# Edge loop of a graph layer: a group's matrix products over three turns, and one ranking step for four tiles in place of two

## The reference

```python
env = 0.5 * (jnp.cos(d * jnp.pi / CUTOFF) + 1.0) * (d < CUTOFF)
rbf = jnp.exp(-0.5 * ((d[:, None] - centers) / (jnp.abs(widths) + EPS_W)) ** 2)
r = _silu(rbf * env[:, None] @ rbf_w1 + rbf_b1) @ rbf_w2 + rbf_b2
W = _silu(r @ filt_w1 + filt_b1)
W = _silu(W @ filt_w2 + filt_b2) @ filt_w3 + filt_b3
msg = (x[col] @ node_w + node_b) * W
agg = jax.ops.segment_sum(msg, row, num_segments=x.shape[0])
...
x = layernorm(x + gated(layernorm(x + agg)))
# second layer: the same edges, x summed forth by src and back by dst,
# weighted with the edge weight, divided by the degrees, then a layer norm
```

## Time and profile before

| | |
|---|---|
| median of 3 runs | 6074.43 us (6072.81 to 6118.61) |
| profiled execution, own time | 6161.62 us |
| profiled execution, span in the trace | 6159.9 us |
| mean granted PE clock over the span | 0.765 |
| busy: PE / PEld / DVE / ACT / POOL | 60% / 45% / 40% / 26% / 56% |

### The profile page before, as it was taken

One profiled execution on the slowest core, in us unless ns is written; L12 is line 12 of the kernel. 1 busy time (PEld: TensorE's weight loads), 2 busy tenths in 40 slices (PEclk: granted clock), 3 DMA queues, 4 the chain that ended last, 5 costly groups with the idle time before them and its releaser, 6 DMA issues. The chain is left out here.

```text
span 6159.9 us, 77269 instructions
## 1 busy us (share of the span) xinstructions
PE 3684.4 (60%) x16362; PEld 2754.2 (45%) x16363; DVE 2437.0 (40%) x7283; ACT 1598.0 (26%) x4213; POOL 3420.9 (56%) x3664
## 2 busy tenths in 40 slices
PE   7677776776766777676899633333333444444443
PEld 5444544444444544444688533333332444443443
DVE  5444444444444444444223622112222544444446
ACT  3333333333333333333466511111111000000000
POOL 2555555555555555555567466666666555555555
PEclk8888888888888888888999865555555776667666
DMA  7322332332332323232599111111111333332333
GB/s 202 102 91 94 99 101 93 96 101 90 96 100 91 99 91 97 92 100 95 178 289 293 44 43 43 44 43 42 43 44 56 89 81 80 82 81 74 80 81 86
DMA packets 466367, 589.69 MB, mean 96 GB/s; under 512 B 71696, under 2 KB 387088, under 8 KB 466320
## 3 DMA queue, kind: packets, MB, share of 16 engines
q0 software_dynamic: 128512, 318.04, 16.6%
q1 hardware_dynamic: 337808, 271.12, 15.1%
HBM read 392.20 MB, written 196.67 MB: 96 GB/s over the span
## 5 line engine op out<-in xcount | busy, mean ns | idle before, releaser
L520 POOL DMA_INDIRECT s_rows<-arena,adr x784 | 769.5, 982 | 1155.2 <-issue 1128.7
L945 PE MATMUL ps<-f3s,arena 128*128 128x256 f32 x3136 | 924.8, 460 | 343.2 <-ACT arena L633 331.3
L573 POOL DMA_INDIRECT arena<-x_half,idx x832 | 800.9, 963 | 581.7 <-DVE idx L1496 305.8
L560 POOL DMA_INDIRECT d_rows<-arena,adr x832 | 816.9, 982 | 534.4 <-ACT adr L757 245.2
L945 PEld LDWEIGHTS ps<-f3s,arena 128*128 128x128 f32 x3136 | 725.1, 237 | 484.7 <-issue 328.7
L512 POOL DMA_INDIRECT arena<-y_rows,idx x784 | 757.6, 966 | 308.9 <-issue 237.4
L1119 PE MATMUL ps<-arena 128*128 128x128 f32 x1664 | 364.1, 386 | 766.4 <-DVE arena L1503 506.9
L934 PE MATMUL ps<-arena,f2s 128*128 128x512 f32 x1568 | 719.0, 602 | 0.0
L1119 PEld LDWEIGHTS ps<-arena 128*128 128x128 f32 x1664 | 312.8, 281 | 811.1 <-issue 810.5
L1330 DVE TENSOR_TENSOR arena<-arena,ps 128x512 f32<-128x512 f32 x392 | 269.1, 686 | 825.7 <-PE ps L945 399.7
L1455 DVE TENSOR_TENSOR arena<-rec,ps 128x512 f32<-128x512 f32 x208 | 142.9, 687 | 977.9 <-remote 845.5
(11 more groups left out here) (217 smaller groups left out, 5532.7 us busy)
## 6 DMA issues: line engine op xcount, KB each, us to landing
arena<-s_rows SPq DMA_DIRECT2D x104, 1048.0 KB, 5.7
arena<-d_rows SPq DMA_DIRECT2D x52, 1040.0 KB
arena<-wrow SPq DMA_DIRECT2D x392, 64.0 KB
arena<-env_row SPq DMA_DIRECT2D x392, 64.0 KB
d_rows<-arena,adr POOLq DMA_INDIRECT x832
arena<-x_half,idx POOLq DMA_INDIRECT x832
s_rows<-tpl_s SPq DMA_DIRECT2D x98, 131.0 KB
arena<-y_rows,idx POOLq DMA_INDIRECT x784
```

The costliest lines, as they stand in the source:

```text
L520: pool.indirect_dma_start(s_rows, bass.IndirectOffsetOnAxis(ap=adr[b][:, t:t + 1], axis=0), msg[b][:, t, :], None).then_inc(scattered[b], 16)
L560: pool.indirect_dma_start(d_rows, bass.IndirectOffsetOnAxis(ap=adr[b][:, t:t + 1], axis=0), drow[b][:, t, :], None).then_inc(scattered_d[b ...
L573: pool.indirect_dma_start(gath2[b][:, t, :], None, x1_half, bass.IndirectOffsetOnAxis(ap=idx[b % 4][:, t:t + 1], axis=0)).then_inc(gathere ...
L945: last = mm(o, s3[:, k, t * P:(t + 1) * P], f3s[:, k, :], start=False, stop=False, skip_group_check=True)
```

## The change

Two things change in the edge loop.

**Order.** PE's turn becomes `layer4(g)`, `layer23(g+1)`, the ranking step of g+2, `layer1(g+2)`, `layer5(g-1)`. The products of one group, which stood in two turns and a bit, now stand in three: layer 1 two turns ahead, layers 2 and 3 one turn ahead, layer 4 in the turn, layer 5 one turn behind. ACT and DVE follow: ACT's turn is `silu3(g)` with `bias_in(g-1)` between its halves, `silu2(g+1)`, `silu1(g+2)`, `radial(g+3)`, then the staging as before; DVE's is `radial_basis(g+2)`, `product(g+2)`, both halves of `messages(g-1)`, `ranked(g+2)`, `one_hot_rank(g+3)`. `s3`, the input of layer 5, gets a second buffer.

**Ranking.** A group's four tiles are ranked in one step of eight products (columns 392, 294, 196, 98, 294, 196, 98, 392) in place of two steps of four (196, 98, 196, 98); one product on DVE over 392 columns replaces two over 196.

```diff
-            def silu3(g):
-                for m in range(2):
-                    act.wait_ge(l4_mm, 2 * g + m + 1)
-                    A(s3[:, m, :], ps[:, 3 + m, :], ACT.Silu, bias=col[:, 5 + m:6 + m]).then_inc(s3_done, 1)
+            def silu3(g, b, m):
+                if m == 0 and not (fixed(g) and g < 2):
+                    act.wait_ge(l5_mm, 2 * g - 2)
+                act.wait_ge(l4_mm, 2 * g + m + 1)
+                A(s3[b % 2][:, m, :], ps[:, 3 + m, :], ACT.Silu, bias=col[:, 5 + m:6 + m]).then_inc(s3_done, 1)
...
             def act_group(g, q, b):
-                silu2(g)
+                silu3(g, b, 0)
+                if not (fixed(g) and g == 0):
+                    bias_in(g - 1)
+                silu3(g, b, 1)
+                if ahead(g, 1):
+                    silu2(g + 1)
                 if ahead(g, 2):
-                    radial(g + 2, q + (b + 2) // 4, (b + 2) % 4)
+                    silu1(g + 2, b)
+                if ahead(g, 3):
+                    radial(g + 3, q + (b + 3) // 4, (b + 3) % 4)
                 if ahead(g, 4):
                     stage_idx(g + 4, q + 1, b)
                 if ahead(g, 1):
                     stage_rec(g + 1, q + (b + 1) // 4, (b + 1) % 4)
-                    silu1(g + 1, (b + 1) % 4)
-                bias_in(g)
-                silu3(g)
...
+            def rank_step(g, b):
+                pe.wait_ge(hot_done, g + 1)
+                cur, prev = hot_r[b % 2], hot_r[1 - b % 2]
+                if not (fixed(g) and g == 0):
+
+                    pe.wait_ge(prod_done, g)
+                    mm(ps[:, 7, 0:GT * NB2], after_b[:, :], prev, start=False, stop=False, skip_group_check=True)
+                    for k in range(1, GT):
+                        mm(ps[:, 7, 0:(GT - k) * NB2], ones_b[:, :], prev[:, k:GT, :], start=False, stop=False,
+                           skip_group_check=True)
+                for k in range(1, GT):
+                    mm(ps[:, 7, k * NB2:GT * NB2], ones_b[:, :], cur[:, 0:GT - k, :], start=False, stop=False,
+                       skip_group_check=True)
+                mm(ps[:, 7, 0:GT * NB2], before_b[:, :], cur, start=False, stop=False,
+                   skip_group_check=True).then_inc(rank_mm, 1)
...
             def layer4(g):
                 pe.wait_ge(s2_done, 2 * g + 2)
+                if not (fixed(g) and g == 0):
+                    pe.wait_ge(s3_done, 2 * g)
...
             def pe_group(g, q, b):
-                layer23(g, b)
+                layer4(g)
+                if ahead(g, 1):
+                    layer23(g + 1, b + 1)
                 if ahead(g, 2):
-                    rank_step(g + 2, b, 0)
+                    rank_step(g + 2, b)
+                    layer1(g + 2, b)
                 if not (fixed(g) and g == 0):
-                    layer5(g - 1)
-                if ahead(g, 2):
-                    rank_step(g + 2, b, 1)
-                if ahead(g, 1):
-                    layer1(g + 1, b + 1)
-                layer4(g)
+                    layer5(g - 1, b + 1)
...
-            def product(g, b, h):
-                dve.wait_ge(rank_mm, 2 * g + h + 1)
-                if h == 0 and not (fixed(g) and g == 0):
+            def product(g, b):
+                dve.wait_ge(rank_mm, g + 1)
+                if not (fixed(g) and g == 0):
                     dve.wait_ge(rank_done, g)
-                V.tensor_tensor(prod[:, 2 * h:2 * h + 2, :], hot_r[b % 2][:, 2 * h:2 * h + 2, :],
-                                ps[:, 7, 0:2 * NB2].rearrange("p (t n) -> p t n", t=2), ALU.mult).then_inc(prod_done, 1)
+                V.tensor_tensor(prod[:, :, :], hot_r[b % 2], ps[:, 7, 0:GT * NB2].rearrange("p (t n) -> p t n", t=GT),
+                                ALU.mult).then_inc(prod_done, 1)
...
             def dve_group(g, q, b):
                 if ahead(g, 2):
-                    one_hot_rank(g + 2, b)
-                    product(g + 2, b, 0)
+                    radial_basis(g + 2, b + 2)
+                    product(g + 2, b)
                 if not (fixed(g) and g == 0):
-                    messages(g - 1, q + (b + 3) // 4 - 1, (b + 3) % 4, 0)
+                    for h in range(2):
+                        messages(g - 1, q + (b + 3) // 4 - 1, (b + 3) % 4, h)
                 if ahead(g, 2):
-                    radial_basis(g + 2, b + 2)
-                if not (fixed(g) and g == 0):
-                    messages(g - 1, q + (b + 3) // 4 - 1, (b + 3) % 4, 1)
-                if ahead(g, 2):
-                    product(g + 2, b, 1)
                     ranked(g + 2, b)
+                if ahead(g, 3):
+                    one_hot_rank(g + 3, b + 1)
```

51 lines of the change are left out of this document (21 added, 30 removed).

## The result

The changed kernel takes 5762.55 us (5761.64 to 5771.24, 4 runs), the kernel before, on the same chip, 6086.5 (6072.81 to 6118.61, 4 runs): 324 us less, a ratio of 0.943, 95% interval 0.938 to 0.947. The forecast was 135 less. In a later job the ratio was 0.946.

The account below looks back on a forecast made before the run. The edge loop was taken as bound by POOL's burst, PE's late signal, a message and the next burst. Turns from 14.8 to 14.1 us over 196 turns gave 135 us off 6074, so 5939; range 5585 to 6170.

Parts of the forecast that it names:

- The bound: Edge loop: a circle of POOL's burst, PE's late signal, a message and the next burst; 14.8 us a turn before.
- The held turn: Edge-loop turn with layer 5's signals held until after POOL's burst: 14.2 us, or 13.6 if the first half comes through.
- The doubles: Two POOL bursts without a pause, when layer 5's second half comes through: 24.6 to 32.5 us for two turns.
- The ranking step: PE's 1960 columns in place of 1176: 0.35 us a turn more, hidden in layer 5's spare time, so taken as nothing.
- (a): Edge loop: PE's signals come in time and POOL never waits; 10.3 us a turn, 882 us less, 5190; chance 0.05.
- (b): Edge loop: doubles go well again and again; 12.3 us a turn, 490 us less, 5585; chance 0.13.
- (c): Edge loop: held signals pile up in a new pattern, nothing gained; 14.6 to 15.0 us a turn, 6035 to 6115; chance 0.19.
- (d): Edge loop: at a low PE clock layer 5 ends after the release; 333 us more, 6405; chance 0.18.
- POOL's idle in front of scatters near-equal and no 12 us pauses: Sign on POOL: idle falls to about 3.9 us a turn, near-equal each turn, with few 12 us pauses.
- Messages 0.6 apart after a "remote" idle: Sign on DVE: both messages 0.6 us apart after some 4 us idle, about 2 us after the last gather.
- silu3 turns of 13.5 to 14.3: Sign on ACT: edge-loop turns, read from silu3, lie between 13.5 and 14.3 us.
- Clock 0.9: Sign on PE: the clock in the edge loop is 0.9 or more.

Follow-up runs that it names:

- e1: Kernel before with one ranking step of eight products in place of two of four, in a job without late signals: 1.000 of the kernel before.
- f2: Changed kernel with the ranking in two steps of four products again, in a job with late signals: 5868.58 us, 0.960 of the kernel before.
- g4: Changed kernel with a burst's first two scatters started on the first half of the messages: 5758.35 us, 0.942 of the kernel before.
- g3: Changed kernel with DVE's product, one-hots and next basis moved ahead of the messages: 6082.45 us, 0.994 of the kernel before.
- g1: Changed kernel with a burst's four gathers issued ahead of its four scatters: 5810.55 us, 0.951 of the kernel before.
- g2: Kernel before with a burst's four gathers issued ahead of its four scatters: 6109.15 us, 0.996 of the kernel before.
- f4: Changed kernel without gathers from the fifth group on, sums not the reference's: 5079.13 us, 0.832 of the kernel before.
- h3: Changed kernel with two of a group's four gathers left out from the fifth group on, in a job without late signals: 0.965 of the kernel before.
- e2: Changed kernel with the ranking in two steps of four products again, in a job without late signals: 1.004 of the kernel before.
- e3: Kernel before with POOL also waiting for layer 4 of the next group before scattering, in a job without late signals: 1.000 of the kernel before.
- e4: Changed kernel with the first two scatters started on the first half of the messages, in a job without late signals: 1.004 of the kernel before.
- h1: Changed kernel with POOL waiting on layer 5 between scatters and gathers, in a job without late signals: 1.004 of the kernel before.
- i1: Changed kernel with POOL waiting on layer 5 between scatters and gathers, run again without late signals: 1.006 of the kernel before.

## Why the forecast missed: the bound held, two terms of the sum did not

The direction and the bound were right; the gain was put at 135 us and is 324. The step that failed is the sum: "Most turns 14.2 or 13.6, some doubles at 12.3 to 16.3 a turn: I take 14.1." The turn measured is 12.8 us.

**The bound: right where it was read, and not everywhere.** Late signals under POOL's bursts set the turn, in before and after. In four jobs they did, in three there were none. The Trainium skill's page SBUF — State Buffer, section "SBUF: two separate sides", has it that the ports of the engines and those of the transfers cannot contend with each other. The three jobs agree: in e1, with 47% of the transfer engines' time in use, nothing of PE's is late. In the four, signals come 3.3 us late as above; what is late there is a completion, and no run shows that it is a matter of ports. The Trainium skill's page Perfetto Trace Analysis, section "Tensor Engine Instruction (MATMUL, LD_WEIGHTS)", says that PE's recorded end is estimated and that the signal follows only when PSUM has acknowledged the bytes. The 3.3 us lie between these two by our rows, and PE had by then begun layer 4 (at 1237.48); the rows can't show whether the writing or the signal is what is late.

**The held turn: mis-sized, 14.2 against 13.2.** This is the first term that failed: "2.3 + 9.9 + 2.0 = 14.2". The burst (9.94) and the way from the last message to POOL (1.71) were right. The forecast has the second message start 2.0 + 0.6 = 2.6 us after the last gather; in 88 held turns it starts 1.51 us after it on the median, and these turns take 13.16 us. I had read the 2.0 off a turn of before in which only the second half was held, and then put the 0.6 us pitch of the messages on top. In 73 held turns of before the second message, measured the same way, starts 1.83 us after the last gather. So 0.8 of the 1.1 us was counted wrongly from the start: one row stood for a distribution, and the pitch was added to a number that held it. The other 0.3 is not explained.

**A kind of turn was missing.** The sum knows held turns, with the release 2.0 us after the last gather, and doubles. 52 of 170 turns of the changed kernel are of a third kind, the short turn: pauses of 1.0 to 2.3 us, the second message at the very end of the last gather (median 0.00 us from it), 11.65 us a turn. There layer 5 ended 9.5 us into the burst on the median, and 37 of the 52 signals are less than 1 us late. They come too late for a double, since POOL starts 1.71 us after a message, and too soon for a held turn. The forecast put layer 5 at 7.9 us in every turn; at the full clock it is 7.3 to 7.4, and the median of all is 9.0. When such a signal passes is not settled by its place: in f2, 83 second halves end 9.0 to 9.9 us into the burst, and 80 of them are held, by 2.0 us on the median.

**The doubles: I kept them at 24.6 to 32.5 us a pair; they became few, and cheap.** This is the second failed term, 24.6 to 32.5 being the 12.3 to 16.3 a turn of the sum. 44 became 13, and a pair costs 26.8 in place of 32.0. That is 1.3 of the 2.02 us. I saw that a double costs 32.5 us for two turns but took "some" of them along without asking how many second halves would still come through early enough; and no row that I had chose between my two prices.

**The ranking step: priced at nothing, worth some 1.5% in the new order.** Its 0.35 us of PE cost nothing that shows. Not seen was that one step in place of two takes a held signal out of the turn: DVE's second product before waited for it. That this is the way in which it gains was not tested.

**The rivals.** (a) is what happens where nothing is late. (b) comes nearest in g4, as triples of 12.7 us a turn. (c) is what g3 does, with 14.4 us a turn. (d), PE's clock, did not slow the kernel, but its sign came: in 39 of 170 turns PE's records of layer 5 end after the last gather. 12 of them are second turns of doubles, 14.9 to 16.1 us long; the other 27 take 12.1 us on the median, less than a held turn (11.8 to 14.9, and 13.0 in the one above).

**What was to be seen.** POOL's idle in front of scatters near-equal and no 12 us pauses: the long ones are gone, but the idle is 2.8 us and not 3.9, and of two sizes, 1.75 and 3.26. Messages 0.6 apart after a "remote" idle: in 41 turns of 170 only; mostly the first half comes through earlier. silu3 turns of 13.5 to 14.3: no, 12.8. Clock 0.9: 0.89. Later stages unchanged: 13 us of 399.

**What stays open.** What on the chip holds the completions, and why only in some jobs. The runs exclude the kind of transfer (g1, g2); they don't separate POOL's issuing from the bytes. The packets of POOL's queue end 1.1 to 1.5 us after the burst's last instruction, so the two ends lie close together: signals that are released after that instruction come 0.3 us before the last packet's end in the changed kernel, 0.1 after it in the kernel before and 0.5 after it in g1 (medians). In the turn shown the release, at 1240.93, comes while the last gather's packets run (1240.86 to 1241.67). So waiting for the last byte is not the whole of it. Nor was it tested why turns of 11 to 12 us come up in the changed kernel (52 and 37 of 170 in its two traces) and hardly in f2 (5 of 170); by the counts, that is where the one ranking step gains in the new order.

## What to carry to other kernels

Where an engine's signals are released only near the end of another engine's burst, finishing the work earlier need not shorten the turn (g3), and a wait that holds the bursting engine back can be a gain (4% here, with one wait). Don't judge a double burst by its being there: add up the pair. Here a pair took 32.0 us before, 32.7 in f2, 29.2 in g3, 26.8 in the changed kernel and 25.3 in g4, against 26.4 for two held turns. By the timelines of before and g3, what makes a pair dear is the work that stands between the release and the next burst; no run took only that work away. Size a lag from its distribution over all turns, not from the turn in the timeline, and look for a second kind of turn. And try such a change under both conditions: it was worth 5% in one, and in the other its near variants cost 0.4 to 0.6%.

## What the runs showed that was not expected

- The kernel before took 4711 to 4717 us in three jobs and 6074 to 6158 in the others. In those three no half of layer 5 that DVE stood waiting for was more than 0.14 us late (nine traces), and the clock in the edge loop was 1.00; otherwise it was 0.84 to 0.92, but for f4 without gathers, which has 1.00 too. Both kinds occurred under one chip number (6117.57 and, in a later job, 4716.72), so these runs don't say that it is a property of the chip.
- Where completions come late, a second burst without a pause held one signal for 12.2 us (g3), against the 3.3 us of the turn with one burst above.
- With fewer transfers on POOL the turn, from burst to burst, is 9.33 us whether the job was of the one kind (f4, four transfers a turn, 6117 us before) or the other (h3, six, 4717 before). So PE itself is as fast in both.
- In the jobs with late signals POOL also stands still for 1.67 us between the first and the second scatter of every eleventh group, after 88 transfers (16 of 170 turns in the changed kernel, 15 before). In e1 to e4, h1 and i1 it never does, nor in f4. What it is, no run tells.
